# Attention scores by 64-row matmuls of 128 columns, one head on each half of TensorE's rows

## The chip, the cores and the metric

The program runs on one core of a Trainium2 chip. The metric is device time in microseconds of one execution. The core has TensorE (matmuls and, beside them, the loads of its stationary operand), VectorE, ScalarE, GpSimd and the DMA queues, which SyncE mostly feeds. In the profile they are PE and PEld, DVE, ACT, POOL and SP.

## The reference

The input x holds 32 batches of 128 x 1024 in float32. Stage one adds to each batch a product with a 128 x 128 matrix gathered by an index. Stage two is causal attention over those 128 rows with 16 heads of 64, added to its input:

```python
x = x + einsum('bct,bcd->bdt', x, weights[index])
q, k, v = x Wq^T, x Wk^T, x Wv^T            # (32, 16 heads, 128, 64)
scores = einsum('bhqd,bhkd->bhqk', q * min(cond, 4), k) / 8
attn = softmax(where(causal, scores, lowest))
x = x + einsum('bhqk,bhkd->bhqd', attn, v) Wo^T
```

## The kernel before

Every float32 product is made of three matmuls (`three`, lines 767 to 770). An operand is split into a high half, rounded by a copy to the type fp32r (ScalarE), and a low half, the rest (VectorE or GpSimd). The three are high by high, high by low and low by high, added up in one bank of PSUM. Each matmul instruction stands behind a weight load of its own, a record of PEld.

The kernel has three stretches: the first stage with the V projection (to about 382 us of the span), the attention (from 382 to about 1270 us, with the first eight output rows at its end), and the rest of the output projection. The attention is cut into 64 groups n. A group is four batches (u = 0 to 3, `GB = 4`) and two of the 16 heads (128 columns of Wq and Wk). It has

- 8 steps of the q block and 8 steps of the k block. A step is one `three` of 512 columns (the four batches beside each other) into a bank of `PJ`. Two heads of 64 lie on the 128 rows of the result;
- the split of q (`QH` on ScalarE, `QL` on VectorE) and of k (`KH`, line 1105; `KL`, line 1295), which read the bank;
- four score units U = 4n + u. A unit is one `three` with Q's 128 columns of batch u as the stationary operand and 256 columns of K as the moving one. K is padded for it: `KH` and `KL` are `[128, 4, 256]`, and in each unit's 256 columns the first 128 hold head 0 on rows 0 to 63 and zeros on rows 64 to 127, the last 128 hold head 1 on rows 64 to 127 and zeros above. So a matmul over all 128 rows gives both heads' scores side by side. Units 0 and 1 share bank SC[0], units 2 and 3 share SC[1]. GpSimd writes the zeros once (lines 1399 to 1406), and each split of k writes two instructions of 64 rows;
- the softmax: mask and scale (L1308) and row maximum (L1314) on VectorE, exp on ScalarE (L1118), reciprocal on VectorE, normalisation on GpSimd (L1438), a turn of 32 x 32 blocks (L1185), ten DMAs that put the turned blocks in place (`sp_move_p`, L1640), and a split of the result (L1128 and L1441) some 20 steps later;
- 8 matmuls of 256 columns with V (`pe_values`, L873), whose banks ScalarE and VectorE read.

The order is written out by hand. Time is counted in steps of TensorE (a `three` of 512 columns); `sc_at.put`, `mask_at.put` and the like give each piece a step, and each engine's program goes through the steps and issues what is due. So each engine has its pieces in a fixed order, and semaphores tie the engines together. Scores of a group stand 5 steps behind the end of its k block (`a = done + 5`), the units 0 and 1 at step a, the units 2 and 3 at a + 1. The masks stand at a + 1 for units 0 and 1 and at a + 3 for units 2 and 3. The next q and k blocks are in between.

Of the kernel before, what the change touches and what calls it, by code (L numbers as in the profile page):

```python
# [45 lines left out]
def cond_attention(nc, x, idx, cond, w0, wq, wk, wv, wo, mask_d, ident_d, out):  # L46
# [14 lines left out]
    with ExitStack() as ctx:  # L61
        def sb(name, shape, dt=f32, where=ctx):
            return where.enter_context(nc.sbuf_tensor("t_" + name, shape, dt))

        def pb(name):
            return ctx.enter_context(nc.psum_tensor("p_" + name, [128, 512], f32))
# [93 lines left out]

        with nc.sbuf_tensor("t_LATE", [128, 4, 512], f32) as tile:
            LATE = tile
        KH = sb("KH", [128, GB, 256], f32r)
        KL = sb("KL", [128, GB, 256], f32r)
        QH = sb("QH", [128, T], f32r)
        QL = sb("QL", [128, T], f32r)

# [10 lines left out]
        OL = sb("OL", [128, 512], f32r)  # L178

        PJ = [pb(f"PJ{n}") for n in range(3)]  # L180
        SC = [pb("SC0"), pb("SC1")]
        PV2 = ctx.enter_context(nc.psum_tensor("p_PV", [128, 2, 512], f32))
        PV = [PV2[:, 0, :], PV2[:, 1, :]]
        LP = pb("LP")
# [188 lines left out]
        for j in range(NGRP):  # L373
            t0 = T_ATT + STEPS * j
            for c in range(NC):
                n = 4 * j + c
                for i, kind in enumerate("qk"):
                    block(kind, n)
                    for d in range(DC):
                        step_at.put(t0 + 16 * c + 8 * i + d, (kind, n, d))  # L380
                done = t0 + 16 * c + 8
                late = 2.5 if n else 0
                q_ev.put(done + late, n)
                ql_ev.put(done + late + 1, n)
                done += 8
                kh_ev.put(done + 0.25, n)
                kl_ev.put(done + 1, n)
                a = done + 5
                for u in range(GB):
                    k = u // 2  # L390
                    sc_at.put(a + k, GB * n + u)
                    mask_at.put(a + 1 + 2 * k, GB * n + u)
                    exp_at.put(a + (2, 3, 4, 5)[u], GB * n + u)
                move_at.put(a + 10, n)
                for k in range(2):
                    P = 2 * n + k
                    recip_at.put(a + 4 + 2 * k, P)
                    norm_at.put(a + 4.25 + 2 * k, P)
                    turn_at.put(a + 7.5 + 1.5 * k, P)
                    last = n == 4 * NGRP - 1  # L400
                    half_at.put(a + (20 if last else 25.25) + 0.5 * k, P)
                    ptl_at.put(a + (20.75 if last else 26) + 1.5 * k, P)
                    v = a + (27.25 + 3.25 * k if last else 29 + 4.5 * k)
                    own = v + (1.75 if n >= 4 * NGRP - 2 else (1.75, 8.5)[k])
                    for z in range(2):
                        pv_at.put(v, 2 * P + z)
                    other_at.put(v + 0.75, P)
                    own_at.put(own, P)
                    at_at.put(own + 1.25, P)

            if j and j != NG:
                for i in range(8):
                    X_load.put(t0 - STEPS + ((25.5, 41.5)[i // 4] if j in (1, NG + 1) else (9.5, 25.5, 41.5)[i // 3]), (j, i))
            for k in range(2):
                V_load.put(t0 + ((-11, 2.75)[k] if j == 0 else -38.5 + 16 * k if j == NG else -6.5), (j, k))
            for u in range(GB):
                v_split.put(t0 + ((17, 19, 27.75, 28.75)[u] if j == 0 else 3.75 + u + 14 * (u // 2)), (j, u))
# [82 lines left out]
        def x1_stores(z):  # L500
            return sum(x_slot(k) == z for k in range(B))
# [66 lines left out]
        def products_turned(bb, h):  # L568
            return sum(not turned_by_dve(k) for k in range(bb)) * 2 + h + 1
# [183 lines left out]
        def pe_wait_bank(kind, item):  # L753
            old = before[kind, item]
            if old is None:
                return
            kind, i = old
            if kind == "q":
                pe.wait_ge(dve_q, i + 1)
            elif kind == "k":  # L760
                pe.wait_ge(dve_k, 2 * i + 2)
            elif kind == "v":
                pe.wait_ge(act_v, i + 1)
            else:
                pe.wait_ge(dve_out, i + 1)

        def three(bank, lh, ll, rh, rl, first, last, goes_on=False):
            pe.matmul(bank, lh, rh, start=first, stop=False, skip_group_check=goes_on)  # L768
            pe.matmul(bank, lh, rl, start=False, stop=False, skip_group_check=goes_on)  # L769
            return pe.matmul(bank, ll, rh, start=False, stop=last, skip_group_check=goes_on)  # L770
# [79 lines left out]
        def pe_scores(U):  # L850
            n, u = divmod(U, GB)
            cols = slice(u * 128, (u + 1) * 128)
            if u == 0:
                pe.wait_ge(dve_k, 2 * n + 2)
            if U == 0:
                pe.wait_ge(act_v, 2 * GB + NP - 2)
                pe.wait_ge(dve_g, 5 * (NP - 2))
            z = u // 2
            three(SC[z][:, 256 * (u % 2):256 * (u % 2) + 256], QH[:, cols], QL[:, cols], KH[:, u, :], KL[:, u, :], True, True).then_inc(pe_sc, 1)

        def pe_values(U):
            n, u, z = U // GB, U % GB, U % 2
# [179 lines left out]
        def act_program():  # L1042
            for tick in range(T_START * TICK, (T_OUT + 4) * TICK):
# [52 lines left out]
                for n in kh_ev(tick):  # L1096
                    act.wait_ge(pe_k, n + 1)
                    if n:
                        act.wait_ge(pe_sc, 4 * n)
                    else:  # L1100
                        act.wait_ge(pool_z, 3)
                    pj = PJ[bank_of["k", n]][:].rearrange("p (b s) -> p b s", b=GB)
                    for h in range(2):
                        r = slice(64 * h, 64 * h + 64)
                        act.activation(KH[r, :, 128 * h:128 * h + 128], pj[r], ACT.Copy).then_inc(act_k, 1)  # L1105
                for n in q_ev(tick):
                    act.wait_ge(pe_q, n + 1)
                    if n:
# [117 lines left out]
        def dve_program():  # L1226
# [6 lines left out]
            for tick in range(T_START * TICK, (T_OUT + 4) * TICK):  # L1233
# [54 lines left out]
                    dve.wait_ge(act_p, m + 1)  # L1288
                    dve.tensor_tensor(low, raw, high.bitcast(f32), ALU.subtract).then_inc(dve_p, 1)
                for n in kl_ev(tick):  # L1290
                    pj = PJ[bank_of["k", n]][:].rearrange("p (b s) -> p b s", b=GB)
                    for h in range(2):
                        r, k = slice(64 * h, 64 * h + 64), slice(128 * h, 128 * h + 128)
                        dve.wait_ge(act_k, 2 * n + h + 1)
                        dve.tensor_tensor(KL[r, :, k], pj[r], KH[r, :, k].bitcast(f32), ALU.subtract).then_inc(dve_k, 1)  # L1295
                for n in ql_ev(tick):
                    dve.wait_ge(act_q, n + 1)
                    dve.tensor_tensor(QL[:], PJ[bank_of["q", n]][:], QH[:].bitcast(f32), ALU.subtract).then_inc(dve_q, 1)
                for U in mask_at(tick):
                    n, u = divmod(U, GB)  # L1300
                    bb = GROUP[n // NC] * GB + u
                    if n and u == 0:
                        dve.wait_ge(dve_t, 2 * n)
                    dve.wait_ge(pe_sc, GB * n + 2 * (u // 2) + 2)
                    if U == 0:
                        dve.wait_ge(l_mask, 16)
                        dve.wait_ge(dve_beta, 1)
                    dve.scalar_tensor_tensor(  # L1308
                        out=PP[:, u], in0=SC[u // 2][:, 256 * (u % 2):256 * (u % 2) + 256].rearrange("p (h k) -> p h k", h=2), scalar=beta[:, bb:bb + 1],
                        in1=mask[:].unsqueeze(1).to_broadcast([128, 2, 128]), op0=ALU.mult, op1=ALU.add).then_inc(dve_s, 1)  # L1310
                for U in mask_at(tick):
                    u = U % GB
# [83 lines left out]
        def pool_program():  # L1396
            pool.memset(PRH[:].bitcast(f32), 0.0).then_inc(pool_z, 1)
            for tick in range(T_START * TICK, (T_OUT + 4) * TICK):
                if tick == (T_ATT - 20) * TICK:
                    pool.wait_ge(pe_b, products_turned(B, -1))  # L1400
                    pool.wait_ge(dve_tt, half_turns(B, -1))
                    pool.wait_ge(s_p, 32 * 16)
                    for z in range(3):
                        pool.wait_ge(s_x1[z], 16 * x1_stores(z))
                    pool.memset(KH[:].bitcast(f32), 0.0).then_inc(pool_z, 1)
                    pool.memset(KL[:].bitcast(f32), 0.0).then_inc(pool_z, 1)
                if tick == (T_ATT - 8) * TICK:
                    pool.wait_ge(dve_S, 4 * (NP - 2))
                    pool.memset(PT[:], 0.0).then_inc(pool_z, 1)
# [218 lines left out]
        def sp_move_p(n):  # L1628

            sp.wait_ge(dve_t, 2 * n + 2)  # L1630
            if n == 0:
                sp.wait_ge(pool_z, 5)
            elif n >= 2:
                sp.wait_ge(pool_pt, 2 * n - 2)
            if n == 59:
                sp.wait_ge(pool_z, 6)
            for i in range(4):
                for j in range(i + 1):
                    src = turned(n)[32 * i:32 * i + 32, j].rearrange("a u q -> a (u q)")
                    sp.dma_start(p_tile(n)[32 * j:32 * j + 32, i, :], src).then_inc(l_P, 16)  # L1640
# [190 lines left out]
```

## Time and profile before

| | us |
|---|---|
| median of 3 runs | 1558.75 (1557.72 to 1561.19) |
| the profiled execution, its own time | 1558.96 |
| its span in the profile | 1557.5 |
| TensorE busy in the span | 1547.1 |
| VectorE, ScalarE, GpSimd busy | 1034.9, 840.9, 866.6 |
| mean granted TensorE clock | 0.998 |

The profile has one record for every instruction. The end of a matmul's record is modelled and overlaps the next one, so TensorE's pace is read from the starts of its records and not from their lengths. Busy TensorE says only that no gap was left between records.

### The profile page before, as it was taken

Reading aid. Unit: us, or ns where it says so; the run is one execution under the profiler, and the core shown is the slowest. Engines: PE = TensorE matmul, PEld = TensorE weight load, DVE = VectorE, ACT = ScalarE, POOL = GpSimd, SP = SyncE. Lnnn points to the kernel's source line nnn. Section 1 sums busy time; section 2 is a strip of 40 time slices with the busy share of each in tenths; the row PEclk is TensorE's granted clock in tenths of the full one; section 3 lists DMA queues with packets and bytes.
Section 4 is the critical chain, followed back from the end, with each engine's and each line's share of the span. In section 5 each row is a group of like instructions: output and inputs, shape, how many; then the busy total and the mean of one; then the engine's idle time right before and its main releaser. Section 6 shows DMA issues by size and latency. Waiting matters only on the chain.

```text
span 1557.5 us, 23477 instructions
## 1 busy us (share of the span) xinstructions
PE 1547.1 (99%) x7459; PEld 1302.0 (84%) x7459; DVE 1034.9 (66%) x1891; ACT 840.9 (54%) x2286; POOL 866.6 (56%) x752
## 2 busy tenths in 40 slices
PE   9999999999999999999999999999999989999999
PEld 7888888888888888888888888888888878888887
DVE  5867677664477777777767777777777644555553
ACT  6666566652466666666655666666666622222220
POOL 1555665662365566557655576575577545555552
PEclk9999999999999999999999999999999999999999
DMA  9968988866766677767677466677665696444442
GB/s 324 335 230 278 319 307 296 294 254 231 273 190 198 201 214 209 205 184 191 182 240 229 147 179 202 194 200 200 180 188 157 237 366 226 162 168 163 162 167 83
DMA packets 192300, 341.46 MB, mean 219 GB/s; under 512 B 23986, under 2 KB 116402, under 8 KB 185010
## 3 DMA queue, kind: packets, MB, share of 16 engines
q1 hardware_dynamic: 191026, 331.59, 66.2%
q10 hardware_dynamic: 1152, 8.39, 1.4%
q8 instruction: 59, 0.97, 0.3%
q14 instruction: 63, 0.52, 0.1%
HBM read 184.70 MB, written 134.22 MB: 205 GB/s over the span
## 4 chain that ended last, share of the span: by engine, by line
PE 95%; DVE 2%; DMA 1%; SPq 1%; POOL 0%; issue 0%; ACT 0%; DVEq 0%; POOLq 0%
PE p_PJ L768 22%; PE p_PJ L769 22%; PE p_PJ L770 22%; PE p_SC L770 6%; PE p_SC L769 6%; PE p_SC L768 6%; PE p_PV L873 4%; PE p_LP L768 1%; PE p_PV L768 1%; PE p_PV L770 1%; PE p_PV L769 1%; PE p_LP L770 1%; PE p_LP L769 1%; DVE t_WSL L1285 1%; DVE t_TS L1281 1%; DMA out<-t_xr 0%
## 5 line engine op out<-in xcount | busy, mean ns | idle before, releaser
L769 PE MATMUL p_PJ<-t_XL,t_WH 128*128 128x512 f32 x1008 | 394.2, 391 | 0.0
L768 PE MATMUL p_PJ<-t_XH,t_WH 128*128 128x512 f32 x1008 | 394.2, 391 | 0.0
L770 PE MATMUL p_PJ<-t_XH,t_WL 128*128 128x512 f32 x1008 | 392.1, 389 | 0.0
L1118 ACT ACTIVATE t_PP<-t_PP,t_st 128x128 f32<-128x128 f32 x512 | 199.5, 391 | 174.9 <-DVE t_st L1314 173.3
L1438 POOL TENSOR_TENSOR t_PP<-t_PP,t_st 128x512 f32<-128x512 f32 x128 | 133.2, 1041 | 205.8 <-DVE t_st L1318 205.8
L770 PEld LDWEIGHTS p_PJ<-t_XH,t_WL 128*128 128x128 f32 x1008 | 189.3, 188 | 40.5
L768 PEld LDWEIGHTS p_PJ<-t_XH,t_WH 128*128 128x128 f32 x1008 | 190.0, 188 | 33.8
L769 PEld LDWEIGHTS p_PJ<-t_XL,t_WH 128*128 128x128 f32 x1008 | 190.0, 188 | 32.3
L1332 DVE TENSOR_REDUCE t_AT<-p_PV 64x256 f32<-64x512 f32 x252 | 171.3, 680 | 24.5 <-ACT t_AC L1136 12.1
L1444 POOL TENSOR_TENSOR t_AT<-t_AT,t_AC 128x256 f32<-128x256 f32 x126 | 117.1, 929 | 126.2 <-DVE t_AT L1332 126.2
L1441 POOL TENSOR_TENSOR t_PS<-t_PT,t_PS 128x512 fp32r<-128x512 f32 x122 | 157.6, 1292 | 0.0
L1308 DVE SCALAR_TENSOR_TENSOR t_PP<-p_SC,t_beta,t_mask 128x256 f32<-128x256 f32 x256 | 111.5, 477 | 44.1 <-PE p_SC L770 44.1
L1427 POOL TENSOR_TENSOR t_xl<-t_XT,t_xh 128x512 fp32r<-128x512 f32 x56 | 81.5, 1456 | 104.1 <-ACT t_xh L978 103.1
L1318 DVE RECIPROCAL t_st<-t_st 128x4 f32<-128x4 f32 x128 | 22.8, 178 | 142.0 <-ACT t_PP L1118 142.0
L1105 ACT ACTIVATE t_KH<-p_PJ 64x512 fp32r<-64x512 f32 x128 | 75.7, 592 | 47.0 <-PE p_PJ L770 45.4
L1135 ACT ACTIVATE t_AC<-p_PV 64x256 f32<-64x256 f32 x128 | 48.8, 381 | 95.3 <-PE p_PV L873 93.8
L1118 ACT ACTIVATION_READ_ACCUMULATOR t_PP<-t_PP,t_st 128x1 f32 x512 | 95.5, 187 | 0.0
L1295 DVE TENSOR_TENSOR t_KL<-p_PJ,t_KH 64x512 fp32r<-64x512 f32 x128 | 88.2, 689 | 11.0 <-ACT t_KH L1105 7.1
L1432 POOL TENSOR_TENSOR t_VV<-t_VX,t_VV 128x512 fp32r<-128x512 f32 x64 | 81.4, 1293 | 25.0 <-ACT t_VV L1082 25.0
L1314 DVE TENSOR_REDUCE t_st<-t_PP 128x2 f32<-128x256 f32 x256 | 94.1, 408 | 0.0
L873 PE MATMUL p_PV<-t_PS,t_VV 128*128 128x256 f32 x512 | 82.8, 285 | 4.0 <-POOL t_PS L1441 4.0
L873 PEld LDWEIGHTS p_PV<-t_PS,t_VV 128*128 128x128 f32 x512 | 75.1, 192 | 9.6 <-POOL t_PS L1441 4.4
(259 smaller groups left out, 3597.7 us busy)
## 6 DMA issues: line engine op xcount, KB each, us to landing
t_XH<-xth_scratch SPq DMA_DIRECT2D x56, 512.0 KB, 6.4
t_XL<-xtl_scratch SPq DMA_DIRECT2D x56, 512.0 KB, 6.7
t_PT<-t_TB SPq DMA_DIRECT2D x580, 32.0 KB, 2.3
v_scratch<-t_VR SPq DMA_DIRECT2D x64, 256.0 KB, 4.6
xth_scratch<-t_XH SPq DMA_DIRECT2D x16, 1024.0 KB, 4.5
xtl_scratch<-t_XL SPq DMA_DIRECT2D x16, 1024.0 KB, 6.8
t_VX<-v_scratch SPq DMA_DIRECT2D x32, 512.0 KB, 5.6
at_scratch<-t_AT SPq DMA_DIRECT2D x126, 128.0 KB, 3.4
```

Of the source, the lines that this page charges most:

```text
L768: pe.matmul(bank, lh, rh, start=first, stop=False, skip_group_check=goes_on)
L769: pe.matmul(bank, lh, rl, start=False, stop=False, skip_group_check=goes_on)
L770: return pe.matmul(bank, ll, rh, start=False, stop=last, skip_group_check=goes_on)
L873: mm = pe.matmul(PV2[:, z, 256 * h:256 * h + 256], VV[j % 2][:, u, 2 * c + h, :], moving, start=True, stop=True)
L1118: act.activation(PP[:, u, h, :], PP[:, u, h, :], ACT.Exp, bias=st[:, 0, u, h:h + 1], scale=1.0, accum_out=st[:, 1, u, h:h + 1]).then_inc(a ...
L1295: dve.tensor_tensor(KL[r, :, k], pj[r], KH[r, :, k].bitcast(f32), ALU.subtract).then_inc(dve_k, 1)
L1308: dve.scalar_tensor_tensor(out=PP[:, u], in0=SC[u // 2][:, 256 * (u % 2):256 * (u % 2) + 256].rearrange("p (h k) -> p h k", h=2), scalar=b ...
L1314: dve.tensor_reduce(st[:, 0, u, :], PP[:, u], AX, ALU.max, negate=True).then_inc(dve_m, 1)
L1332: dve.tensor_reduce(at_tile(P)[r], both, AX, ALU.add).then_inc(dve_M, 1)
L1438: pool.tensor_tensor(pp, pp, r, ALU.mult).then_inc(pool_n, 1)
L1441: pool.tensor_tensor(p_half(P, 1), p_raw(P), p_half(P, 0).bitcast(f32), ALU.subtract).then_inc(pool_pt, 1)
L1444: pool.tensor_tensor(at_tile(P), at_tile(P), AC[:, P % 2], ALU.add).then_inc(pool_at, 1)
```

## The change

The scores of a unit become six matmuls in place of three. Each takes 64 rows (one head) and 128 columns; the two heads of a product alternate, head 0 on rows 0 to 63 into the first of two banks, head 1 on rows 64 to 127 into the second. The stationary operand is again Q's 128 columns, now 64 rows of it. K needs no zeros: `KH` and `KL` are `[128, 512]`, split by one instruction each, and the two memsets go. A tensor `SPARE` keeps the addresses of what follows. All four units write both banks, so all stand at step a, and the mask of each waits for the last of the four. The mask reads its two heads from the two banks.

```diff
-        KH = sb("KH", [128, GB, 256], f32r)
-        KL = sb("KL", [128, GB, 256], f32r)
+        KH = sb("KH", [128, T], f32r)
+        KL = sb("KL", [128, T], f32r)
+        sb("SPARE", [128, 2, T])
...
-        SC = [pb("SC0"), pb("SC1")]
+        SC2 = ctx.enter_context(nc.psum_tensor("p_SC", [128, 2, 512], f32))
+        SC = [SC2[:, 0, :], SC2[:, 1, :]]
...
-                    sc_at.put(a + k, GB * n + u)
+                    sc_at.put(a, GB * n + u)
...
-            three(SC[z][:, 256 * (u % 2):256 * (u % 2) + 256], QH[:, cols], QL[:, cols], KH[:, u, :], KL[:, u, :], True, True).then_inc(pe_sc, 1)
+            for lh, rh, first, last in ((QH, KH, True, False), (QH, KL, False, False), (QL, KH, False, True)):
+                for h in range(2):
+                    r = slice(64 * h, 64 * h + 64)
+                    mm = pe.matmul(SC2[:, h, cols], lh[r, cols], rh[r, cols], start=first, stop=last)
+            mm.then_inc(pe_sc, 1)
...
-                    for h in range(2):
-                        r = slice(64 * h, 64 * h + 64)
-                        act.activation(KH[r, :, 128 * h:128 * h + 128], pj[r], ACT.Copy).then_inc(act_k, 1)
+                    act.activation(KH[:], PJ[bank_of["k", n]][:], ACT.Copy).then_inc(act_k, 1)
...
-                    for h in range(2):
-                        r, k = slice(64 * h, 64 * h + 64), slice(128 * h, 128 * h + 128)
-                        dve.wait_ge(act_k, 2 * n + h + 1)
-                        dve.tensor_tensor(KL[r, :, k], pj[r], KH[r, :, k].bitcast(f32), ALU.subtract).then_inc(dve_k, 1)
+                    dve.wait_ge(act_k, n + 1)
+                    dve.tensor_tensor(KL[:], PJ[bank_of["k", n]][:], KH[:].bitcast(f32), ALU.subtract).then_inc(dve_k, 1)
...
-                    dve.wait_ge(pe_sc, GB * n + 2 * (u // 2) + 2)
+                    dve.wait_ge(pe_sc, GB * n + GB)
...
-                        out=PP[:, u], in0=SC[u // 2][:, 256 * (u % 2):256 * (u % 2) + 256].rearrange("p (h k) -> p h k", h=2), scalar=beta[:, bb:bb + 1],
+                        out=PP[:, u], in0=SC2[:, :, 128 * u:128 * u + 128], scalar=beta[:, bb:bb + 1],
...
-                    pool.memset(KH[:].bitcast(f32), 0.0).then_inc(pool_z, 1)
-                    pool.memset(KL[:].bitcast(f32), 0.0).then_inc(pool_z, 1)
```

The waits on `dve_k` and `pool_z` are counted anew to match.

## Rows read from the trace of the kernel before

**Rows 1.** Page: busy us, share of the span, instructions.
```profile
PE 1547.1 (99%) x7459; PEld 1302.0 (84%) x7459; DVE 1034.9 (66%) x1891; ACT 840.9 (54%) x2286; POOL 866.6 (56%) x752
```

**Rows 2.** Busy time by stretch of the span, with clock and DMA share.
```profile
core 0: us, PE busy (x) PEld busy (x) DVE busy (x) ACT busy (x) POOL busy (x), PEclk, DMA share, GB/s
397.00:1240.00 843.00, 843.00 (x4301) 720.75 (x4300) 613.79 (x1244) 536.96 (x1684) 511.52 (x458) 1.00 0.67 200
1240.00:1270.00 30.00, 26.05 (x113) 21.50 (x112) 11.57 (x22) 9.25 (x30) 9.96 (x10) 0.89 0.90 323
```

**Rows 3.** Waits of TensorE in the whole span (all that there are).
```profile
PE p_PV L873 <- POOL t_PS L1441: 4.0, 1, 4.0
PE p_PJ L948 <- POOL t_PRH L1397: 1.3, 1, 1.3
PE p_LP L768 <- POOL t_wl L1422: 0.9, 1, 0.9
PE p_LP L768 <- issue: 0.8, 1, 0.8
PE p_PJ L768 <- DVE t_SL L1269: 0.5, 1, 0.5
```

**Rows 4.** Order of time, TensorE, one group's scores: start us, length us.
```profile
811.20 0.28 PE L768 MATMUL p_SC<-t_KH,t_QH 128*128 128x256 f32 x1
811.31 0.28 PE L769 MATMUL p_SC<-t_KL,t_QH 128*128 128x256 f32 x1
811.43 0.28 PE L770 MATMUL p_SC<-t_KH,t_QL 128*128 128x256 f32 x1
...
811.91 0.40 PE L768 MATMUL p_PJ<-t_XH 128*128 128x512 f32 x1
812.14 0.40 PE L769 MATMUL p_PJ<-t_XL,t_XH 128*128 128x512 f32 x1
...
812.61 0.28 PE L768 MATMUL p_SC<-t_KH,t_QH 128*128 128x256 f32 x1
...
813.31 0.64 PE L873 MATMUL p_PV<-t_PS,t_VV 128*128 128x256 f32 x4
```

**Rows 5.** Order of time, TensorE, first and last of 50 matmuls of 512 columns.
```profile
388.20 0.39 PE L769 MATMUL p_PJ<-t_XL,t_WH 128*128 128x512 f32 x1
...
399.30 0.39 PE L770 MATMUL p_PJ<-t_XH,t_WL 128*128 128x512 f32 x1
```

**Rows 6.** All score matmuls of the kernel, first product: length min/median/max ns.
```profile
L768 PE MATMUL p_SC<-t_KH,t_QH x256: 277/280/284, 399.5 to 1239.4; 128*128 128x256 f32 x128
```

**Rows 7.** Order of time, TensorE's matmuls around four transposes of 128 columns.
```profile
153.06 0.39 PE L770 MATMUL p_PV<-t_WSH,t_SL 128*128 128x512 f32 x1
153.29 0.60 PE L902 MATMUL p_LP<-t_ident,t_XT 128*128 128x128 f32 x4
153.65 0.47 PE L768 MATMUL p_PV<-t_WSH,t_SH 128*128 128x512 f32 x1
153.96 0.39 PE L769 MATMUL p_PV<-t_WSL,t_SH 128*128 128x512 f32 x1
```

**Rows 8.** The same stretch, weight loads.
```profile
153.62 0.19 PEld L768 LDWEIGHTS p_PV<-t_WSH,t_SH 128*128 128x128 f32 x1
153.73 0.19 PEld L769 LDWEIGHTS p_PV<-t_WSL,t_SH 128*128 128x128 f32 x1
```

**Rows 9.** Lengths of the transposes: count, min/median/max ns.
```profile
L902 PE MATMUL p_LP<-t_ident,t_XT x68: 270/272/276, 10.8 to 358.1; 128*128 128x128 f32 x68
```

**Rows 10.** Splits of k and q's low half: length min/median/max ns.
```profile
L1105 ACT ACTIVATE t_KH<-p_PJ x128: 573/592/595, 395.6 to 1233.9; 64x512 fp32r<-64x512 f32 x128
L1295 DVE TENSOR_TENSOR t_KL<-p_PJ,t_KH x128: 682/690/698, 396.3 to 1235.1; 64x512 fp32r<-64x512 f32 x128
L1298 DVE TENSOR_TENSOR t_QL<-p_PJ,t_QH x64: 690/691/693, 390.8 to 1231.2; 128x512 fp32r<-128x512 f32 x64
```

**Rows 11.** Waits of the other engines, 420 to 1230 us.
```profile
DVE t_st L1318 <- ACT t_PP L1118: 136.6, 121, 1.4
...
DVE t_PP L1308 <- PE p_SC L770: 37.8, 61, 1.0
```

**Rows 12.** Order of time, GpSimd ahead of the attention.
```profile
368.65 0.95 POOL L1405 MEMSET t_KH<- 128x1024 f32 x1
369.54 0.95 POOL L1406 MEMSET t_KL<- 128x1024 f32 x1
375.79 0.95 POOL L1409 MEMSET t_PT<- 128x1024 f32 x1 [5.30 <-DVE t_SL L1269]
```

More of the change, by code:

```diff
@@ L760, in pe_wait_bank @@
             elif kind == "k":
-                pe.wait_ge(dve_k, 2 * i + 2)
+                pe.wait_ge(dve_k, i + 1)
             elif kind == "v":
@@ L853, in pe_scores @@
             if u == 0:
-                pe.wait_ge(dve_k, 2 * n + 2)
+                pe.wait_ge(dve_k, n + 1)
             if U == 0:
@@ L857, in pe_scores @@
                 pe.wait_ge(dve_g, 5 * (NP - 2))
-            z = u // 2
-            three(SC[z][:, 256 * (u % 2):256 * (u % 2) + 256], QH[:, cols], QL[:, cols], KH[:, u, :], KL[:, u, :], True, True).then_inc(pe_sc, 1)
+            for lh, rh, first, last in ((QH, KH, True, False), (QH, KL, False, False), (QL, KH, False, True)):
[3 more added lines that the diff above has]
+            mm.then_inc(pe_sc, 1)
         def pe_values(U):
@@ L1100, in act_program @@
                     else:
-                        act.wait_ge(pool_z, 3)
-                    pj = PJ[bank_of["k", n]][:].rearrange("p (b s) -> p b s", b=GB)
-                    for h in range(2):
-                        r = slice(64 * h, 64 * h + 64)
-                        act.activation(KH[r, :, 128 * h:128 * h + 128], pj[r], ACT.Copy).then_inc(act_k, 1)
+                        act.wait_ge(s_p, 32 * 16)
+                    act.activation(KH[:], PJ[bank_of["k", n]][:], ACT.Copy).then_inc(act_k, 1)
                 for n in q_ev(tick):
@@ L1290, in dve_program @@
                 for n in kl_ev(tick):
-                    pj = PJ[bank_of["k", n]][:].rearrange("p (b s) -> p b s", b=GB)
-                    for h in range(2):
-                        r, k = slice(64 * h, 64 * h + 64), slice(128 * h, 128 * h + 128)
-                        dve.wait_ge(act_k, 2 * n + h + 1)
-                        dve.tensor_tensor(KL[r, :, k], pj[r], KH[r, :, k].bitcast(f32), ALU.subtract).then_inc(dve_k, 1)
+                    dve.wait_ge(act_k, n + 1)
+                    dve.tensor_tensor(KL[:], PJ[bank_of["k", n]][:], KH[:].bitcast(f32), ALU.subtract).then_inc(dve_k, 1)
                 for n in ql_ev(tick):
@@ L1398, in pool_program @@
             for tick in range(T_START * TICK, (T_OUT + 4) * TICK):
[L1399 to L1404, printed above, removed]
-                    pool.memset(KH[:].bitcast(f32), 0.0).then_inc(pool_z, 1)
-                    pool.memset(KL[:].bitcast(f32), 0.0).then_inc(pool_z, 1)
                 if tick == (T_ATT - 8) * TICK:
@@ L1631, in sp_move_p @@
             if n == 0:
-                sp.wait_ge(pool_z, 5)
+                sp.wait_ge(pool_z, 3)
             elif n >= 2:
@@ L1635, in sp_move_p @@
             if n == 59:
-                sp.wait_ge(pool_z, 6)
+                sp.wait_ge(pool_z, 4)
             for i in range(4):
```

## Prediction

> **What bounds the kernel.** I read the page's first part, then the busy time by stretch, then TensorE's waits. TensorE is busy for 1547.1 of 1557.5 us, VectorE for 66%, ScalarE and GpSimd for little more than half [rows 1]. [...] So what counts is TensorE's own pace. Work saved elsewhere is worth nothing, and each nanosecond added to a score matmul is paid in full.
>
> The pace stands in the starts. In one group, the six matmuls of units 0 and 1 go from 811.20 to 811.91 (0.71 us), those of units 2 and 3 from 812.61 to 813.31 (0.70 us): 1.41 us for 12, or 0.118 us each [rows 4]. A 512-column matmul takes 0.227: the 50 in a row from 388.20 to 399.30 stand 11.10 / 49 apart [rows 5]. The 256 units are alike (277 to 284 ns by record) [rows 6], so the scores cost 64 x 1.41 = 90 us of the span. From 256 to 512 columns the pitch grows by 0.109 us (0.227 - 0.118), that is 0.43 ns a column, which leaves 0.01 us that does not go by columns.
>
> **The change part by part.**
>
> *Matmuls.* 12 of 256 columns become 24 of 128 columns, each with its own weight load: 1536 in place of 768, so TensorE's count goes from 7459 to 8227 [rows 1]. By columns alone, 24 matmuls one after another would take 24 x (0.055 + 0.01) = 1.56 us, and in pairs side by side 0.78 us. [...] The trace has matmuls of 128 columns: the transposes. Four are one record of 0.60 us; with 0.272 us for a single one [rows 9] they start (0.60 - 0.272) / 3 = 0.109 us apart [rows 7], though 128 columns need 0.055. Behind them a load begins at 153.62 and the next at 153.73: 0.11 us for one load of 128 columns of weights. The matmul between (153.65) is 0.47 long in place of 0.39, so it stood 0.08 us until its weights were there [rows 7, 8]. At 256 columns the load just hides behind the matmul before it; at 128 it no longer does. The new matmuls keep a stationary operand of 128 columns, with half the rows.
>
> [...]
>
> No row shows a 64-row operand. Bounds for the 24 matmuls of a group: below, 12 pairs side by side at the pitch of the columns, 12 x 0.065 = 0.78 us (load and stream both halved by the two halves working together); above, 24 at the pitch of a 512-column matmul, 24 x 0.227 = 5.45 us, if short fp32r streams run at a fraction of the rate. Between lie three cases: pairs side by side with both loads at once, 12 x 0.11 = 1.32 us; loads one after another, 24 x 0.109 = 2.62 us; pairs side by side whose stream is slow, 12 x 0.227 = 2.72 us. The nearest rows are the transposes, with one load in front of each 128-column matmul and the loads in single file. I take them: 2.62 - 1.41 = +1.21 us a group, x 64 = +77 us.
>
> *Going over to 64 rows and back.* This happens twice a group, 128 times. Going from matmul to transpose and back costs nothing that I can see: 153.06 to 153.29 is an ordinary 0.23 [rows 7]. The other bound: if the array must run empty, the tail of a record behind its stream (0.39 - 512 x 0.00043 = 0.17 us) and one uncovered load (0.11) are paid, 0.28 us. I take one uncovered load, 0.11 x 128 = +14 us; the bounds are 0 and 128 x 0.28 = 36.
>
> *Splits of k.* ScalarE goes from 2 x 592 ns to one of some 0.6 us, VectorE from 2 x 690 to one like q's 691 [rows 10]: 0.59 and 0.69 us a group, 38 and 44 us over the kernel, hidden behind TensorE, which never waits for them [rows 3]. If that cover were gone, they could return no more than these. K's low half is ready about 1.3 us earlier; nothing waits for that.
>
> *Memsets.* Two of 0.95 us go from GpSimd, which idles 5.30 us behind them anyway [rows 12]. Nothing.
>
> *Order and waits.* Units 2 and 3 stand one step earlier, so a step moves behind them; the sum on TensorE is the same. The first mask waits for all 24 matmuls, 2.6 us from the first of them in place of 0.7. Behind it on VectorE stand the row maxima, the reciprocals and the turns, and for these ScalarE's exp, GpSimd's normalisation and SyncE's ten moves. VectorE waits about 0.6 us for scores in a group now [rows 11] and has (843 - 613.79) / 64 = 3.6 us idle in one [rows 2], plus 0.7 from k and 1.2 from a longer group. The turned probabilities are wanted some 20 steps later. The delay of 1.9 us stays there: nothing. The 4.0 us wait near 1260 [rows 3] hangs on moves behind an output store on SyncE's queue, which shift with TensorE; nothing, by up to 2 us either way.
>
> **Sum.** 1558.96 (profiled execution) + 77 + 14 = 1650. The median of the runs is 0.2 us below that execution, which I leave out. Within 0.2% (3 us) is what a measurement can't tell from no change.
>
> **Rivals.**
>
> *Both halves load and stream together, but going over costs.* For it: the halves have rows and banks of their own. Against: no row shows two loads at once. 12 x 0.11 - 1.41 = -0.09 us a group, -6 us; with one to two bounds of the switch, +14 to +36: 1567 to 1589. [...]
>
> *Faster: the pair at less than 0.118 us.* This is the point that decides: 12 pairs must take less than 1.41 us with the switches. With both loads at once and free switches it gives -6 us, 1553, or -9 at a pitch of 0.107; at the pitch of columns, 12 x 0.065 - 1.41 = -0.63 us, -40 us, 1519. For it: transposes switch freely [rows 7]. Against: a load of 128 columns took 0.11 us, and -40 needs it halved.
>
> *Short streams are slow.* For it: every fp32r matmul in the trace has 256 columns or more, so nothing excludes it. Against: the same. Side by side +1.31 us a group, +84, with switches to +120: 1643 to 1679. One after another (5.45 - 1.41) x 64 = +259: 1818.
>
> *It does nothing:* pairs at 0.11 to 0.12 with free switches end within 3 us of 1559.
>
> **How the numbers follow.** Loads in single file 0.36 (1636 to 1672, from the switch bounds); slow streams in pairs 0.14; together with costly switches 0.22; together with free switches and faster 0.11; no change 0.05; the pitch of columns 0.07; slow and in single file 0.05. Slower: 0.36 + 0.14 + 0.22 + 0.05 = 0.77; faster: 0.18; same: 0.05. The range runs from 1551 (loads together, free switches) to 1679 (slow pairs, full switches); outside are the pitch of columns and the worst case, 0.12. The likeliest case's own range is 1636 to 1672.
>
> **What the profile after would show.** Starts of the score matmuls: single file gives even steps of 0.11 and about 2.6 us from a group's first score to what follows its last; together gives two starts a few hundredths apart and 0.11 to the next pair; slow streams give 0.23 between pairs. A switch shows as a gap ahead of the first 64-row load and behind the last. The 512-column matmuls should keep 0.227, VectorE lose 44 us and ScalarE 38 of busy time, and TensorE gain no waits. The forecast is wrong if loads of the two halves overlap in their records and the pairs step by 0.12 or less, or if VectorE's late masks make TensorE wait at L873.

## The result, and the profile after

The changed kernel took 1578.46 us (median; 1577.19 to 1579.56) against 1559.24 in the same runs before: a ratio of 1.0122 (95% interval 1.0105 to 1.014). It is slower by 19 us, where I had forecast 91.

The page's first part, and the waits of TensorE in the span:

```profile
PE 1564.9 (99%) x8227; PEld 1291.2 (82%) x8227; DVE 990.7 (63%) x1827; ACT 803.4 (51%) x2222; POOL 864.0 (55%) x750
...
PE p_PV L878 <- POOL t_PS L1432: 6.4, 1, 6.4
```

TensorE has its 768 further matmuls, VectorE and ScalarE lost the 44 and 37 us of K's halves, and TensorE still has no long wait but the one near the end [rows 1, 3]. So most of the 20.6 us of span must have come from its own pace. One group's scores, in order of time (the line numbers have moved: L863 is the score matmul, L878 the V product, L1307 the mask, L1331 VectorE's read of the V product):

```profile
819.60 0.39 PE L772 MATMUL p_PJ<-t_XH,t_XL 128*128 128x512 f32 x1
819.92 0.33 PE L863 MATMUL p_SC<-t_KH,t_QH 64*128 64x128 f32 x2
820.08 0.28 PE L863 MATMUL p_SC<-t_KL,t_QH 64*128 64x128 f32 x2
820.19 0.28 PE L863 MATMUL p_SC<-t_KH,t_QL 64*128 64x128 f32 x2
820.30 0.28 PE L863 MATMUL p_SC<-t_KH,t_QH 64*128 64x128 f32 x2
...
821.20 0.28 PE L863 MATMUL p_SC<-t_KH,t_QL 64*128 64x128 f32 x2
821.40 0.49 PE L770 MATMUL p_PJ<-t_XH 128*128 128x512 f32 x1
821.74 0.39 PE L771 MATMUL p_PJ<-t_XL,t_XH 128*128 128x512 f32 x1
```

and the loads of the same stretch:

```profile
819.91 0.19 PEld L863 LDWEIGHTS p_SC<-t_KH,t_QH 64*128 64x128 f32 x2 [0.35 <-issue]
820.02 0.19 PEld L863 LDWEIGHTS p_SC<-t_KL,t_QH 64*128 64x128 f32 x2
...
821.14 0.19 PEld L863 LDWEIGHTS p_SC<-t_KH,t_QL 64*128 64x128 f32 x2
821.40 0.19 PEld L770 LDWEIGHTS p_PJ<-t_XH 128*128 128x128 f32 x1
821.51 0.19 PEld L771 LDWEIGHTS p_PJ<-t_XL,t_XH 128*128 128x128 f32 x1
```

Each record holds both heads: "x2" in 0.19 us for the loads and in 0.28 for the matmuls, as long as a single one (0.19 and 0.27 in c_single). The two halves load together and multiply together, and a pair follows the last by (821.14 - 820.02) / 10 = 0.112 us, the time of one load of 128 columns [rows 8]. Going over shows at both ends. Ahead of the block the first load does not start with the matmul before it, but 0.31 us behind its start (819.91 to 819.60; 0.32 in the median of the 64 groups). In the kernel before, 5748 of the 5795 loads between two 512-column matmuls start within 0.02 us of the matmul ahead of them. By the estimate of 512 x 0.43 = 0.22 us for the stream, from the prediction's 0.43 ns a column, that is 0.09 behind its end; then 0.11 us pass for the load. Behind the block the same again. A record lasts 0.17 us longer than its stream (0.39 for 0.22), so the last stream of the block ends at 821.31; the next load is at 821.40 (0.10 behind that end in the median of the 64), and its matmul is 0.49 long, 0.10 of it, as I read it, a wait for weights: the 41 matmuls of 512 columns in the kernel before whose own load had started less than 0.06 us ahead of them have records of 0.47 to 0.50, the others mostly 0.39 to 0.40.

The sum of a block: from 819.60 to 821.74 are 2.14 us, less the two 512-column matmuls in it (0.454) 1.686 us. 12 pairs take 1.333 of it, so a going-over costs (1.686 - 1.333) / 2 = 0.18 us. The same measure before, in which a group has two blocks of six, starts at this row:

```profile
810.97 0.39 PE L770 MATMUL p_PJ<-t_XH,t_XL 128*128 128x512 f32 x1
```

From there to 812.14 [rows 4] are 1.17 us, less 0.454 0.716, for both blocks 1.43 (the 1.41 of the prediction is the twelve pitches alone). 64 x (1.686 - 1.43) = 16 of the 20.6 us. Some 2 us more stand at a V product: from first score to first score a group takes 13.61 us for 13.33 before (mean of 61 groups in each trace), 0.28 and not 0.25 more. The late mask puts them there, as shown below. The last 2.4 us are the wait at L878 near the end (6.4 for 4.0 us). I don't put it down to the change: the profiled execution of a kernel below (a_early) has 6.3 us there; it took 1561.63 us, but the median of that kernel is that of the kernel before.

### The profile page after: what moved, and what is told of

The parts are those of the page before. It is cut to its first block, busy times and chain, and to the rows that moved or that the text cites. A ratio compares the mean times of both kernels' runs of the same rounds, so it can differ in the third digit from the quotient of the medians.

```text
span 1578.1 us, 24880 instructions
## 1 busy us (share of the span) xinstructions
PE 1564.9 (99%) x8227; PEld 1291.2 (82%) x8227; DVE 990.7 (63%) x1827; ACT 803.4 (51%) x2222; POOL 864.0 (55%) x750
## 4 chain that ended last, share of the span: by engine, by line
PE 94%; DVE 2%; DMA 1%; SPq 1%; issue 0%; ACT 0%; POOL 0%; DVEq 0%; POOLq 0%
PE p_PJ L770 22%; PE p_PJ L772 21%; PE p_PJ L771 21%; PE p_SC L863 6%; PE p_SC L772 4%; PE p_SC L771 4%; PE p_SC L770 4%; PE p_PV L878 4%; PE p_LP L770 1%; PE p_PV L772 1%; PE p_PV L770 1%; PE p_PV L771 1%; PE p_LP L772 1%; PE p_LP L771 1%; DVE t_WSL L1287 1%; SPq L1631 1%
## 5 line engine op out<-in xcount | busy, mean ns | idle before, releaser
L770 PE MATMUL p_PJ<-t_XH,t_WH 128*128 128x512 f32 x1008 | 399.6, 396 | 0.0
L1331 DVE TENSOR_REDUCE t_AT<-p_PV 64x256 f32<-64x512 f32 x252 | 171.2, 679 | 41.6 <-ACT t_AC L1138 29.1
L1307 DVE SCALAR_TENSOR_TENSOR t_PP<-p_SC,t_beta,t_mask 128x256 f32<-128x256 f32 x256 | 111.5, 477 | 95.3 <-PE p_SC L863 95.3
L878 PEld LDWEIGHTS p_PV<-t_PS,t_VV 128*128 128x128 f32 x512 | 74.7, 190 | 25.4 <-issue 12.7
L878 PE MATMUL p_PV<-t_PS,t_VV 128*128 128x256 f32 x512 | 85.7, 289 | 6.6 <-POOL t_PS L1432 6.4
L1187 DVE STREAM_TRANSPOSE t_TB<-t_PP 128x512 f32<-128x512 f32 x116 | 75.1, 686 | 0.0
L1130 ACT ACTIVATE t_PS<-t_PT 128x512 fp32r<-128x512 f32 x122 | 74.3, 619 | 0.0
```

What stands on the lines that cost most here:

```text
L878: mm = pe.matmul(PV2[:, z, 256 * h:256 * h + 256], VV[j % 2][:, u, 2 * c + h, :], moving, start=True, stop=True)
L1307: dve.scalar_tensor_tensor(out=PP[:, u], in0=SC2[:, :, 128 * u:128 * u + 128], scalar=beta[:, bb:bb + 1], in1=mask[:].unsqueeze(1).to_broa ...
L1331: dve.tensor_reduce(at_tile(P)[r], both, AX, ALU.add).then_inc(dve_M, 1)
```

## The experiments

My theory: two loads on different halves cost one, going over costs 0.18 us each way, and nothing else matters. The rivals were the late mask, and other readings of the gaps.

**The order and the wait alone (a_order).** The kernel before with:

```diff
-                    sc_at.put(a + k, GB * n + u)
+                    sc_at.put(a, GB * n + u)
...
-                    dve.wait_ge(pe_sc, GB * n + 2 * (u // 2) + 2)
+                    dve.wait_ge(pe_sc, GB * n + GB)
```

> The kernel before with only the order and the wait of the change: all four score units at step a, and every mask waits for the last of them. Matmuls, padding and splits of k as before. Theory (the loss is on TensorE, at the two goings-over between 128-row and 64-row matmuls in each group): 1559 us, TensorE waits at the first V product of the last group 4.0 us or, if the later mask is behind the 2.4 us that this wait grew by, 6.4 us and 1561 us. Rival (the later first mask or the moved step costs the 19 us): about 1578 us.

1573.67 us, ratio 1.0098 (1.0083 to 1.0114). The rival was nearly right, and I had overlooked it because "idle before" of TensorE's matmuls stays empty. VectorE, weight loads and TensorE in this kernel, in order of time:

```profile
820.16 0.88 DVE L1308 SCALAR_TENSOR_TENSOR t_PP<-p_SC,t_beta,t_mask 128x256 f32<-128x256 f32 x2 [1.35 <-PE p_SC L770]
...
826.66 1.30 DVE L1185 STREAM_TRANSPOSE t_TB<-t_PP 128x512 f32<-128x512 f32 x2
827.88 1.37 DVE L1332 TENSOR_REDUCE t_AT<-p_PV 64x256 f32<-64x512 f32 x2
...
829.36 0.53 PEld L873 LDWEIGHTS p_PV<-t_PS,t_VV 128*128 128x128 f32 x4 [0.37 <-issue]
...
831.99 0.28 PE L768 MATMUL p_SC<-t_KH,t_QH 128*128 128x256 f32 x1
...
833.69 0.88 DVE L1308 SCALAR_TENSOR_TENSOR t_PP<-p_SC,t_beta,t_mask 128x256 f32<-128x256 f32 x2 [1.32 <-PE p_SC L770]
```

The V product's load starts 0.11 us behind the end of L1332 (829.25), for which it waits (`dve_M`); it does so once in nearly every group (59 times between 430 and 1230 us), and in the kernel before twice in all. L1332 stands on VectorE behind the row maxima, two waits for exp and both turns, all behind the mask. So there is a loop: first mask to the end of L1332 9.09 us, to the V load 0.11, to the next scores 2.63, to the next mask 1.70: 13.53 us. These pieces run from mask to mask, so they add up to a group's time in any kernel; what shows that no slack is left in them is the load right behind the end of L1332. In the kernel before, the mask starts 0.98 us behind the first score [rows 4, and the row below], so its loop is 12.8 us, and TensorE's own work of a group is 13.3. The same place there:

```profile
812.18 0.88 DVE L1308 SCALAR_TENSOR_TENSOR t_PP<-p_SC,t_beta,t_mask 128x256 f32<-128x256 f32 x2 [0.63 <-PE p_SC L770]
...
819.89 1.37 DVE L1332 TENSOR_REDUCE t_AT<-p_PV 64x256 f32<-64x512 f32 x2
...
821.76 0.65 PEld L873 LDWEIGHTS p_PV<-t_PS,t_VV 128*128 128x128 f32 x4
821.98 0.64 PE L873 MATMUL p_PV<-t_PS,t_VV 128*128 128x256 f32 x4
822.45 0.40 PE L768 MATMUL p_PJ<-t_XH,t_WH 128*128 128x512 f32 x1
```

L1332 ends at 821.26 and the load comes 0.50 us later: 0.4 us of slack, less than the 0.7 us by which the mask was delayed. The other 3.6 us of idle VectorE lay elsewhere in the loop, in waits for exp and scores, and could not take the delay.

**Which of the two edits (a_early).** Only the first of the two edits of a_order.

> The kernel before with all four score units at step a, but each mask waiting as before (units 0 and 1 for the first two units, 2 and 3 for all). Theory (the mask's wait for all four, 0.7 us more from a group's first score matmul to its first mask, makes the loop of mask, softmax, L1332, V product and next scores longer than TensorE's own work): 1559 us, groups of 13.3 us, no gap at the V products. Rival (the step that moved behind the scores is what costs): 1573 us, groups of 13.55 us.

1559.13 us, ratio 0.9998 (0.9989 to 1.0007). The wait is the cause of the 15 us; the moved step costs nothing. (Its one wait of TensorE behind the opening is the 6.3 us mentioned above.)

**No going-over, 128 rows and columns (f12_norows).** The changed kernel with

```diff
                 for h in range(2):
-                    r = slice(64 * h, 64 * h + 64)
-                    mm = pe.matmul(SC2[:, h, cols], lh[r, cols], rh[r, cols], start=first, stop=last)
+                    mm = pe.matmul(SC2[:, h, cols], lh[:, cols], rh[:, cols], start=first, stop=last)
```

and `range(1)` in place of `range(2)`.

> The changed kernel with each unit's six 64-row matmuls replaced by three 128-row ones of 128 columns (Q's and K's columns of the batch over all 128 rows, so the two heads are summed into one score, and the second bank isn't written): no going-over at all, half the matmuls. Theory (a 128-column load sets the pitch at 0.111 us whether it is alone or one of a pair, and the rest of the loss is the goings-over): 12 x 0.111 = 1.33 us a group in place of 1.69, 64 x 0.36 = 23 us under the changed kernel, 1555 us, 5 us under the kernel before. Rival (short fp32r streams of 128 columns over all rows run slower than their load, 0.227 each): 12 x 0.227 = 2.72 us a group, 1642 us. Rival (the gaps are there without a change of rows): 1578 us.

1564.37 us, ratio 1.0036 (1.0022 to 1.005). The matmuls step by 0.111 us as the theory has it:

```profile
813.83 0.27 PE L862 MATMUL p_SC<-t_KH,t_QL 128*128 128x128 f32 x1
813.94 0.27 PE L862 MATMUL p_SC<-t_KH,t_QH 128*128 128x128 f32 x1
```

but the time is 9 us over the forecast: the late mask is still in it, and the loop of 13.4 us (first score to first score) is longer than TensorE's 13.25.

**The same pitch with the early mask (g_head0).** The kernel before, `KH[:, u, 0:128]` and `KL[:, u, 0:128]` into the first 128 columns of each unit's place.

> The kernel before with 128 of the 256 moving columns in each score matmul, so the second head's scores are left out; order, waits and the 128-row form as before. Theory (a load of 128 columns is the pitch, 0.111 us, and with the early mask nothing else bounds a group): 64 x 12 x 0.007 = 5 us under the kernel before, 1553 to 1554 us. Rival (something else holds a group at 13.3 us): 1559 us. Rival (short streams are slow): 1640 us.

1553.04 us, ratio 0.9961 (0.9947 to 0.9974): the forecast of both the pitch and the loop. Between this and f12_norows lie 11 us. The two differ in the mask's wait, in the moved step, which costs nothing (a_early), and in the form of K, whose splits TensorE doesn't wait for; so I put the 11 us down to the late mask.

**Four goings-over (b_split).** The changed kernel with `sc_at.put(a + k, ...)`.

> The changed kernel with units 2 and 3 back at step a + 1, so a group goes over to 64 rows and back twice, 4 goings-over in place of 2. Theory (each costs 0.18 us wherever it stands): 64 x 0.36 = +23 us, 1601 us. Rival (the 0.32 us ahead of a group's first 64-row load is its wait for k's low half, the one behind the last the queue of instructions): the second block has no such wait, so at most one gap more, 1578 to 1590 us.

1640.22 us, ratio 1.0523 (1.0507 to 1.0539): 39 us over my theory's 1601, and outside the rival's range too. The profile shows two causes apart:

```profile
835.46 0.39 PE L772 MATMUL p_PJ<-t_XH,t_WL 128*128 128x512 f32 x1
835.78 0.33 PE L863 MATMUL p_SC<-t_KH,t_QH 64*128 64x128 f32 x2
...
836.39 0.28 PE L863 MATMUL p_SC<-t_KH,t_QL 64*128 64x128 f32 x2
836.59 0.50 PE L770 MATMUL p_PJ<-t_XH,t_WH 128*128 128x512 f32 x1
...
837.16 0.39 PE L772 MATMUL p_PJ<-t_XH,t_WL 128*128 128x512 f32 x1
837.48 0.33 PE L863 MATMUL p_SC<-t_KH,t_QH 64*128 64x128 f32 x2
```

The steps are 0.32 and 0.20 us at both blocks, also at the second, which waits for no semaphore: the price of a going-over is 0.18 us at the second block as at the first. The other 39 us I put down to the loop: the mask now waits for a second block behind a whole step, and a group takes 14.6 us. V products waited for L1331 61 times, 0.48 us each on average:

```profile
PE p_PV L878 <- DVE t_AT L1331: 29.4, 61, 0.5
```

**Neighbours on the same half (c_single).** The 12 matmuls of head 0, then the 12 of head 1.

> The changed kernel with another order of the same 24 matmuls of a group: the 12 of head 0 (rows 0 to 63) first, then the 12 of head 1, so neighbours share their rows. Theory (what makes a pair cost one load of 0.111 us is that neighbours lie on different halves): 24 or 23 loads in single file, +11 or 12 x 0.111 x 64 = +78 to +85 us, 1656 to 1663 us. Rival (loads are pulled ahead whatever the order, or two loads of the same half are as cheap as 0.055 us each because only 64 rows are loaded): no more than +5 us, 1578 to 1583 us.

1636.85 us, ratio 1.0501 (1.0485 to 1.0517).

```profile
820.48 0.27 PE L867 MATMUL p_SC<-t_KH,t_QH 64*128 64x128 f32 x1
820.60 0.27 PE L867 MATMUL p_SC<-t_KL,t_QH 64*128 64x128 f32 x1
820.71 0.27 PE L867 MATMUL p_SC<-t_KH,t_QL 64*128 64x128 f32 x1
820.71 0.38 PE L867 MATMUL p_SC<-t_KH,t_QH 64*128 64x128 f32 x2
```

On one half the steps are 0.11 each: single file, and the 64 rows did not load faster than the 128 of f12_norows (0.111). But the first three of head 1 started early, beside the last of head 0 ("x2" at 820.71), so the block has between 20 and 21 steps and not 24: hence 58 us over the changed kernel and not 78.

**256 moving columns (d_cols256)** and **64 stationary columns (e_stat64)**, in the changed kernel:

```diff
# d_cols256
+            two = slice(min(u, 2) * 128, min(u, 2) * 128 + 256)
-                    mm = pe.matmul(SC2[:, h, cols], lh[r, cols], rh[r, cols], start=first, stop=last)
+                    mm = pe.matmul(SC2[:, h, two], lh[r, cols], rh[r, two], start=first, stop=last)
# e_stat64
+            part = slice(u * 128, u * 128 + 64)
-                    mm = pe.matmul(SC2[:, h, cols], lh[r, cols], rh[r, cols], start=first, stop=last)
+                    mm = pe.matmul(SC2[0:64, h, cols], lh[r, part], rh[r, cols], start=first, stop=last)
```

> The changed kernel with 256 moving columns (those of the next batch as well) in each 64-row matmul, so each writes over a neighbour's scores and the result is of other scores. Theory (the two halves stream at the same time, and the load sets the pair's 0.111 us): pairs 0.118 apart, 12 x 0.007 x 64 = +5 us, 1584 us. Rival (the streams of the halves take turns): pairs 0.22 apart, 12 x 0.11 x 64 = +85 us, 1663 us.

> The changed kernel with 64 stationary columns in each score matmul (scores of the first 64 queries of each batch alone, the others left out). Theory (a load goes by its columns): pairs 0.065 apart in place of 0.111, 0.55 us less a group on TensorE, and the time falls until the loop behind the late mask bounds the group: 1560 to 1570 us. Rival (a load has a fixed price, or 64 rows halve it already): pairs still 0.111 apart, 1578 us.

d_cols256 took 1586.04 us, ratio 1.0176 (1.016 to 1.0191); e_stat64 1538.48, ratio 0.9869 (0.9854 to 0.9884). Score matmuls of the two, each kernel by itself:

```profile
823.63 0.28 PE L864 MATMUL p_SC<-t_KL,t_QH 64*128 64x256 f32 x2
...
824.81 0.29 PE L864 MATMUL p_SC<-t_KH,t_QL 64*128 64x256 f32 x2
```

```profile
826.53 0.22 PE L864 MATMUL p_SC<-t_KH,t_QL 64*64 64x128 f32 x2
...
827.07 0.22 PE L864 MATMUL p_SC<-t_KH,t_QL 64*64 64x128 f32 x2
```

Twice the moving columns step by 1.18 / 10 = 0.118 us and not by 0.22: the streams of the halves didn't take turns. Half the stationary columns step by 0.54 / 9 = 0.060: the pitch of the changed kernel was the load, and a load of 64 columns took no more than 0.060. It may take less, since the 128-column streams fill some 0.055 of that by themselves (an estimate from the 0.43 ns a column of the prediction). The 40 us of e_stat64 are 64 x 12 x (0.111 - 0.060) = 39. That it would stick at 1560 to 1570 was wrong: as I read it, shorter scores shortened the loop as well.

**VectorE's read moved ahead of the turns: eight kernels, and a miss.** To open the loop I moved L1332 (in `own_at`) from 8.5 to 5.25 steps behind its V products, in a_order, the changed kernel, b_split and f12_norows. `at_at.put(own + 1.25, P)` moved GpSimd's addition and the store with it:

```diff
-                    own = v + (1.75 if n >= 4 * NGRP - 2 else (1.75, 8.5)[k])
+                    own = v + (1.75 if n >= 4 * NGRP - 2 else (1.75, 5.25)[k])
```

> The kernel before with the order and wait of the change (as in the run that took 1573.7 us), and one piece of VectorE moved: its read of the second pair of V products (L1332 in the kernel before) stands 5.25 steps behind them in place of 8.5, so ahead of both turns of the new group's probabilities. Theory (the later mask delays what stands in front of that read in VectorE's order, and the next V product waits for the read): 1559 us, no gap in front of the V products. Rival (the V products wait for GpSimd's low half of the probabilities or for a bank): 1573 us still.

> The changed kernel with the same piece of VectorE moved. Theory (of its 19 us some 17 are the goings-over less the shorter pairs, on TensorE alone, and 4 are V products that wait for VectorE): 1574 us, 4 us under the changed kernel; the 0.32 and 0.20 us steps at the goings-over stay. Rival (the goings-over are cheap and the late mask is the loss, since the order alone cost 15 us): 1560 us or below.

> The changed kernel with four goings-over a group (units 2 and 3 at step a + 1), which took 1640 us, with the same piece of VectorE moved. Theory: only the two further goings-over are left, 64 x 2 x 0.18 = 23 us over the changed kernel with the moved piece, 1597 us. Rival (a going-over costs 0.48 us, (1640 - 1578) / 128, and the wait on VectorE is its effect and not its own cause): 1636 to 1640 us.

> The kernel with three 128-row matmuls of 128 columns a unit (both heads summed into one score, second bank not written), which took 1564.4 us, with the same piece of VectorE moved. Theory: 12 x 0.111 = 1.33 us of scores a group against 1.41 before, and nothing waits: 5 us under the kernel before, 1554 us. Rival (a 128-column load costs more than its pitch shows): 1559 to 1564 us.

They took 1623.68, 1627.35, 1690.23 and 1612.98 us, some 50 each over the kernels without it. The loads' waits in a_own:

```profile
PEld p_PV L873 <- POOL t_PS L1441: 76.8, 63, 4.8
```

GpSimd has a fixed order too: its addition, which waits for L1332, now stood ahead of the split of the turned probabilities, and the V products waited for that. So I put `at_at` back (v + 8.5 + 1.25) and left only the read moved.

> The kernel before with the order and wait of the change and VectorE's read of the second V products 3.25 steps earlier, as in the run that took 1623.7 us, but with GpSimd's addition (L1444) and the store behind it left at their old step. In that run the addition had moved too, ahead of GpSimd's first split of the turned probabilities (L1441), and the V products waited for that split. Theory (in the order of the change the V product waits only for the read): no gap in front of the V products, 1559 us. Rival (TensorE, the softmax and the V products close a loop that the moved piece only shifts): a wait for L1441 stays, 1565 to 1574 us.

> The changed kernel with the read moved and GpSimd's order as it was. Theory: the goings-over less the shorter pairs stay, 64 x 0.27 = 17.5 us over 1558.8, the wait of the V products (3 to 4 us) is gone: 1575 us, 3 to 4 us under the changed kernel. Rival (the late mask is most of the loss): 1565 us or less.

> The changed kernel with four goings-over a group, the read moved and GpSimd's order as it was. Theory: 64 x 2 x 0.18 = 23 us over the kernel with two goings-over and the same move, 1598 us, if the softmax keeps up; where the mask still comes too late, up to 1640 us, and then the steps at the goings-over (0.32 and 0.20 us) tell the price. Rival (a going-over costs 0.48 us): 1636 to 1640 us with no wait in front of the V products.

> Three 128-row matmuls of 128 columns a unit (both heads summed into one score, second bank not written), the read moved and GpSimd's order as it was. Theory: 64 x (1.33 - 1.41) = -5 us against the kernel before: 1554 us. Rival (the chain behind the mask bounds the group by itself at 13.3 us): 1559 us or more.

1612.22, 1615.15, 1627.37 and 1606.81 us. Waits of TensorE in a_own2, and VectorE's splits of Wo there:

```profile
PE p_SC L768 <- DVE t_KL L1295: 32.7, 48, 1.2
...
L1338 DVE TENSOR_TENSOR t_OL<-t_xr,t_OH 128x512 fp32r<-128x512 f32 x32 | 43.4, 1356 | 0.0
```

In a_order the same 32 pieces took 693 ns each. They stand between the turns and K's low half, and with the read moved they took 1356, 0.66 us more in front of K's low half, for which the scores then waited, 48 times; 48 is also the number of these pieces (32 of L1338, 16 of L1289). All 48 overlap GpSimd's split L1441 there. In a_order the same 48 overlap GpSimd's addition L1444 and took 0.7, so it is not GpSimd at work as such. That this split and VectorE's slow each other I take from the coincidence, and did not test it. None of the eight ran at its forecast; b_own2 alone lies where its theory still allowed it (up to 1640). They say nothing on the loss of the changed kernel, only how little room its order has; and that the late mask reaches TensorE by way of L1332 stays a reading of the traces, since no kernel in which that way was opened ran without another wait. b_own2 against b_split (1627 for 1640) is the one case in which the move helped.

## Why the prediction was wrong

The direction and the range held; the size did not: +19 us for +91. The range went from faster to 120 us slower, so that it held says little, and that the kernel came out slower is owed to the goings-over and not to the loads from which I forecast it. Both signs of being wrong that I had named came: the pairs step by 0.112 us, and late masks delay loads at the V product. By its steps:

- *What bounds the kernel* held as far as it went: TensorE's pace [rows 1, 3]. That "each nanosecond" of it counts and nothing else does was too simple. A loop over the mask, L1332 and the V product stood 0.5 us behind TensorE's own work.
- *Matmuls*: the step that failed. I priced 24 loads in single file, from the transposes, which all use the same rows: 2.62 us a group, +77 us. That the load sets the pace of 128-column matmuls held: the 256-column matmuls stood 0.118 us apart (before), those of 128 columns 0.111 (f12_norows, as the loads), and those with half the stationary columns 0.060 (e_stat64). That a load of 64 rows takes as long as one of 128 was my estimate, and c_single shows it (0.11). But the halves loaded together, and 12 pairs took 1.33 us: -0.08 a group, -5 us where I had +77. That single file costs 0.11 a load was right where loads share their rows (c_single); I gave it 0.36, and the case of pairs with costly switches, 1567 to 1589 us, in which the result lies, 0.22. The trace shows both parts of that case: two loads in 0.11 us, and the next load 0.09 us behind the end of the stream.
- *Going over* was 0.18 us, within my bounds of 0 and 0.28 and above the 0.11 that I took: 128 x 0.18 = +23 us in place of 14. It consists of one load (0.11) that no stream covered and some 0.09 us behind the end of the stream, less the 0.01 (0.227 - 0.22) that a matmul has beside its stream anyway. (-5 and +23 are 18 and not 16, since 0.02 us of each group's blocks stand before as well.) Transposes were no model for this: they keep all 128 rows [rows 7].
- *Splits of k* and *memsets*: right, 44 and 37 us of other engines' time bought nothing.
- *Order and waits*: "The delay of 1.9 us stays there: nothing" was wrong. The delay was 0.7 us (1.67 in place of 0.98 from first score to first mask), and by itself, in the kernel before, it cost 15 us (a_order against a_early). I had compared it with VectorE's whole idle time and not with the slack of the piece in its order that TensorE waits for next.
- In the changed kernel most of that cost hides: TensorE's own group is 13.33 + 0.25 = 13.58 us, and the loop is just as long or a little longer, for a group takes 13.61. Two causes of 16 and 15 us overlap and give 19 with the wait near the end, so neither may be added to the other. With free goings-over the changed kernel would, by my estimate, have come to f12_norows, 1564 us, and still been slower than before.
- *Short streams are slow*: excluded, 128 columns ran at the pitch of their load, 0.112 us in pairs (after) and 0.111 over all rows (f12_norows).
- A slip in the rival *Faster*: at a pitch of 0.107 it gives 12 x 0.107 - 1.41 = -0.13 us a group, -8 and not -9 us. The range's 1551 has it right.

The same two places after the change show that the loop was just closed. L1331 ends at 830.67 and the load follows at 830.78. The first matmul is still in time, 0.23 us behind the one before it, but the four take 0.53 us (830.85 to 831.38) where they took 0.47 before (821.98 to 822.45). The load follows as closely 59 times, as in a_order:

```profile
821.59 0.87 DVE L1307 SCALAR_TENSOR_TENSOR t_PP<-p_SC,t_beta,t_mask 128x256 f32<-128x256 f32 x2 [1.41 <-PE p_SC L863]
...
829.30 1.37 DVE L1331 TENSOR_REDUCE t_AT<-p_PV 64x256 f32<-64x512 f32 x2
...
830.78 0.55 PEld L878 LDWEIGHTS p_PV<-t_PS,t_VV 128*128 128x128 f32 x4 [0.20 <-issue]
830.85 0.69 PE L878 MATMUL p_PV<-t_PS,t_VV 128*128 128x256 f32 x4
831.38 0.39 PE L770 MATMUL p_PJ<-t_XH,t_WH 128*128 128x512 f32 x1
...
833.51 0.33 PE L863 MATMUL p_SC<-t_KH,t_QH 64*128 64x128 f32 x2
```

No version of the whole computation beat the kernel before. What is left to gain by pairs is 64 x 12 x 0.007 = 5 us, with goings-over for nothing and an early mask. The changed kernel with an early mask was not tried. With the two banks of the pairs such a mask would read banks that the later units still write, and no run shows what that does; with four banks it would not. TensorE's own 16 us more would, by my estimate, keep it slower than the kernel before all the same.

## What to carry to other kernels

Zeros in the moving operand cost next to nothing here, since the weight load behind which they hide (0.111 us) is nearly as long as the pitch of the 256-column matmuls (0.118): halving the moving columns of the score matmuls gained 6 us of 1559 (g_head0), because the stationary operand kept its width. Count how often a block of 64-row matmuls is entered and left, here at 0.18 us each, before counting what it saves inside. And when a wait is widened, follow the waiting engine's order to the first piece that the bounding engine waits for, and compare the delay with the slack at that piece, read from the end of the piece to the load that follows it; the idle time of an engine is not its slack.

## What was not expected of the hardware

- Two 64-row loads on different halves of the rows took 0.11 us together, as one of 128 rows did (after, f12_norows); on the same half 0.11 each (c_single). With 64 stationary columns it was at most 0.06 (e_stat64).
- Loads of the other half were pulled ahead of earlier loads in the program's order: in c_single three matmuls of head 1 ran beside the last of head 0 (records of "x2" at 820.71, 820.88 and 820.99 us).
- Between 128-row and 64-row matmuls no load was started until some 0.09 us behind the end of the stream by my estimate of the stream, both going in (load 0.32 us behind the start of the last 512-column matmul, median of 64 in after, of 128 in b_split) and coming back (step of 0.20 us in both).
- Waits for a semaphore left the idle time of TensorE's matmuls at zero, since the ends of their records are modelled: a_order is 15 us slower, and its trace shows that as idle time only in the loads, as "issue" in front of the V products (22.9 us in 61 waits, up to 0.7, of which part is hidden).
